# Gated cross-attention block: attention scores with bias kept in their PSUM banks instead of an SBUF score tile

## The reference, cut to what matters

```python
q = jnp.einsum('bfd,dnh->bfnh', x, Wq) * H ** (-0.5)
k = jnp.einsum('btd,dnh->btnh', src, Wk)
v = jnp.einsum('btd,dnh->btnh', src, Wv)
hbias = jax.nn.relu(dist[..., None] @ Wth + bth)
qs_bias = (hbias @ Wto + bto)[..., 0]
logits = jnp.einsum('btnh,bfnh->bnft', k, q)
logits = logits + bias + qs_bias[:, None]
w = jax.nn.softmax(logits, axis=-1)
out = jnp.einsum('bnft,btnh->bfnh', w, v)
```

## Time and profile before

| what | value |
|---|---|
| median of 3 runs | 1392.51 us (1392.48 to 1393.23) |
| span of the profiled execution, first to last instruction | 1391.1 us |
| what lies around the span, against the median | 1.4 us |
| busy share of the span, PE / DVE / ACT / POOL | 90% / 88% / 76% / 60% |
| mean granted TensorE clock over the span | 0.968 |

### The profile page before, as it was taken

How to read it: one execution, slowest core, us unless ns; L and a number is a source line. 1 busy time by engine, 2 the same in 40 slices (tenths; PEclk the granted TensorE clock), 3 DMA queues, 4 the chain that set the end, 5 groups by cost and what they waited for, 6 DMA issues and landing times.

```text
span 1391.1 us, 39815 instructions
## 1 busy us (share of the span) xinstructions
PE 1246.5 (90%) x11184; PEld 1035.3 (74%) x11184; DVE 1221.8 (88%) x4922; ACT 1062.8 (76%) x3353; POOL 833.3 (60%) x889
## 2 busy tenths in 40 slices
PE   1599989898989899998989898989898999799998
PEld 1377878787878787787778787878777877677776
DVE  4899989898989899998989898989898988579886
ACT  4588868787878788787878787868687866478886
POOL 3677767676767677776767676767676753111110
PEclk9799999999999999999999999999999999999999
DMA  5201000102110100021100000111101000000000
GB/s 152 67 7 31 15 27 12 29 12 76 44 31 12 31 12 22 20 67 39 35 16 16 25 13 29 57 48 27 31 12 42 12 12 9 5 23 19 23 14 9
DMA packets 69115, 41.04 MB, mean 30 GB/s; under 512 B 14840, under 2 KB 63872, under 8 KB 68992
## 3 DMA queue, kind: packets, MB, share of 16 engines
q1 hardware_dynamic: 68992, 39.84, 9.9%
HBM read 23.29 MB, written 1.05 MB: 17 GB/s over the span
## 4 chain that ended last, share of the span: by engine, by line
PE 23%; issue 23%; DVE 23%; ACT 18%; POOL 2%; DVEq 1%; DMA 1%; ACTq 0%; SPq 0%; POOLq 0%
ACT prob L802 10%; DVE bias_acc L951 4%; PE L L688 4%; ACT relu_z L785 4%; PE O L552 3%; PE M L582 3%; DVE score L998 3%; DVE qT L1123 3%; DVE hid L1073 3%; PE M L762 2%; DVE st L1016 2%; PE M L628 2%; PE T L695 2%; PE M L560 2%; ACT probT L809 1%
## 5 line engine op out<-in xcount | busy, mean ns | idle before, releaser
L802 ACT ACTIVATE prob<-score,nmax 128x128 f32<-128x128 f32 x1024 | 396.6, 390 | 182.4 <-DVE nmax L998 182.2
L1396 POOL TENSOR_TENSOR prob<-prob,rinv 128x512 f32<-128x512 f32 x256 | 293.5, 1146 | 232.1 <-DVE rinv L1006 229.7
L951 DVE SCALAR_TENSOR_TENSOR bias_acc<-relu_z,cst,bias_acc 128x512 f32<-128x512 f32 x370 | 339.1, 917 | 9.7 <-ACT relu_z L785 0.2
L785 ACT ACTIVATE relu_z<-dist_g,cst 128x512 f32<-128x512 f32 x386 | 295.0, 804 | 17.2 <-DMA cst<-cst_all 16.9
L998 DVE CUSTOM_DVE_ANT_0 score<-L,bias 128x128 f32<-128x128 f32 x1024 | 233.6, 281 | 4.0 <-PE L L528 1.5
L802 ACT ACTIVATION_READ_ACCUMULATOR prob<-score,nmax 128x1 f32 x1024 | 193.3, 189 | 0.0
L1391 POOL TENSOR_TENSOR sd<-mv,half 128x1 f32<-128x1 f32 x128 | 105.5, 824 | 120.3 <-DVE mv L1018 117.6
L538 PE MATMUL T<-ident,prob 128*128 128x128 f32 x1024 | 164.4, 285 | 4.9 <-POOL prob L1396 4.0
L552 PEld LDWEIGHTS O<-probT,v 128*64 128x64 f32 x2048 | 109.3, 136 | 60.0 <-issue 52.4
L582 PE MATMUL M<-wv,ctxT 128*128 128x512 f32 x256 | 144.1, 645 | 7.8 <-DVE hid L1073 5.1
L528 PE MATMUL L<-kT,qT 64*128 64x128 f32 x2048 | 148.7, 285 | 0.0
(11 more groups left out here) (134 smaller groups left out, 2282.8 us busy)
## 6 DMA issues: line engine op xcount, KB each, us to landing
dist_g<-in_fside_BxSxS SPq DMA_DIRECT2D x16, 256.0 KB, 2.8
mask_g<-in_mask_Bx1x1xS_ff SPq DMA_DIRECT2D x16, 256.0 KB, 3.3
ctxT<-ctxT_all SPq DMA_DIRECT2D x64, 64.0 KB, 1.9
xs<-x_all SPq DMA_DIRECT2D x64, 64.0 KB, 1.8
x_all<-xs SPq DMA_DIRECT2D x64, 64.0 KB, 1.8
wk<-in_L_xattn_Wk SPq DMA_DIRECT2D x4, 512.0 KB, 3.6
wv<-in_L_xattn_Wv SPq DMA_DIRECT2D x4, 512.0 KB, 4.7
wq<-in_L_xattn_Wq SPq DMA_DIRECT2D x4, 512.0 KB, 5.1
```

The lines of the kernel that those rows point to most:

```text
L785: nc.scalar.activation(relu_z[:, z_slot(g, k), :], dist_g[:, :, :], ACT.Relu, bias=cst[:, C_BTH + k:C_BTH + k + 1], scale=cst[:, C_WTH + k ...
L802: last = nc.scalar.activation(prob[:, c, m, :], score[:, c, m, :], ACT.Exp, bias=nmax[:, c, m:m + 1], scale=-1.0, accum_out=rsum[:, c, m:m ...
L951: vec.scalar_tensor_tensor(out=bias_acc[:, :], in0=relu_z[:, z_slot(g, k), :], scalar=weight, in1=bias_acc[:, :], op0=ALU.mult, op1=ALU.ad ...
L1396: gp.tensor_tensor(prob[:, c, :, :], prob[:, c, :, :], rinv[:, c, :].rearrange("p (m o) -> p m o", o=1).broadcast_to([P, 4, P]), ALU.mult) ...
```

## The change

The scores with the bias are written back in place, into the bank that they came from; the exponential reads them there; the SBUF tile `score` (8 KB a partition) is gone. PE may write the banks again only when the exponential has read them, so its wait at L524 goes from `scored` to `exp_done`, with the same count.

```diff
-        score = sb("score", [P, QUADS, 4, P])
...
-                wait(pe, scored, after(g, i, 4, 2 * octet - 1))
+                wait(pe, exp_done, after(g, i, 4, 2 * octet - 1))
...
                 for m in range(4):
-                    last = nc.scalar.activation(prob[:, c, m, :], score[:, c, m, :], ACT.Exp, bias=nmax[:, c, m:m + 1],
+                    last = nc.scalar.activation(prob[:, c, m, :], L[c % 2][:, m * P:(m + 1) * P], ACT.Exp, bias=nmax[:, c, m:m + 1],
                                                 scale=-1.0, accum_out=rsum[:, c, m:m + 1])
...
-                    last = vec.tensor_tensor_reduce(out=score[:, c, m, :], in0=L[c % 2][:, m * P:(m + 1) * P], in1=bias[:, i % GROUP, :],
+                    last = vec.tensor_tensor_reduce(out=L[c % 2][:, m * P:(m + 1) * P], in0=L[c % 2][:, m * P:(m + 1) * P], in1=bias[:, i % GROUP, :],
                                                     scale=-1.0, scalar=BIG, op0=ALU.add, op1=ALU.min,
                                                     accum_out=nmax[:, c, m:m + 1])
```

## The result

The changed kernel takes 1406.33 us (median of 4 runs, 1403.92 to 1414.29), the kernel before, run beside it, 1392.49 us (4 runs, 1386.82 to 1393.23). The two medians are 13.8 us apart, which is 1.0%, where 1404 us was predicted. The ratio on record is 1.013, with a 95% interval of 1.0093 to 1.0167: slower beyond noise, but the size of the loss is known only to some 13 to 23 us. Lines of the file after the removed tile are one lower than before: the scores are L527 instead of L528, the exponential L801, DVE's score instruction L997.

What follows compares the result with a forecast made beforehand. DVE was taken to set the pace, PE having about 0.4 us to spare a step. A loss of 0.7 us a group over 16 groups, 11.2 us on 1391.1, plus 1.4, gave 1404 us; 8-in-10 range 1386 to 1440.

Steps and rivals of the forecast that it cites:

- the first half of the mechanism: Before the octet-1 scores: PE stands until ACT's exponentials of quad 1 are done, 0.60 us in every step.
- The terms of the sum: DVE's added standing in steps 0, 1 and 2 of a group: 0.3 + 0.2 + 0.2 = 0.7 us; step 3 nothing.
- five signs: PE idle 0.6 us before octet-1 scores; exponentials 0.35 apart; score instructions 0.21; DVE waiting for `wo`; steps 1, 2 at 16.7.
- The standing of PE: Before the octet-1 scores, PE waits for ACT's exponentials of quad 1: 0.60 us, in every step.
- The exponential from PSUM: ACT's exponentials of a quad: 0.35 us apart instead of 0.39, a gain of 0.04 each, 0.16 a quad.
- DVE's write to PSUM: DVE's score instructions: no change from 0.21 us apart, with -0.04 and +0.04 us an instruction as ends.
- Rival (b): DVE's score write to PSUM is dear: at +0.04 us each, 0.64 us a step, about 1435 us; chance 0.22.
- DVE sets the pace, PE follows with about 0.4 us to spare: In steps of 16.5 us, DVE sets the time; PE is without work for 0.38 and 0.41 us in steps 1 and 2.
- The wait of DVE for `wo`: Before DVE's residual: PE's late projection `wo` makes DVE stand 0.2 us in steps 1 and 2.
- The turn of the loop: In step 3, PE's 4.27 us without work take its lateness away, so the change costs nothing there.
- Rival (a): PE's own 0.4 us of slack a step swallows the moved wait: no difference, 1395 us; chance 0.18.
- Rival (c): DVE's score write to PSUM is cheaper: at -0.04 us each, 11 us faster in all, 1381 us; chance 0.15.

Runs made afterwards that it cites:

- the wait alone: The kernel before, SBUF tile kept, with only PE's wait moved from `scored` to `exp_done`: 1408.97 us against 1391.78, ratio 1.0133.

## Why the prediction was right, point by point, and where it was off

The direction and the first half of the mechanism held: the time came out 2.3 us above the forecast, well inside its range. The terms of the sum did not hold as well. Of the five signs that were to show the forecast right, two came: PE's standing and the shorter exponentials. The score instructions did not stay at 0.21 us, DVE did not wait for `wo`, and the steps came to 16.9 us instead of 16.7.

**The standing of PE** was right in place, releaser and size: 0.57 us measured (row and median), 0.60 predicted, and it came in 63 of 64 units. So was its cause, the loop through `apply`, the copy of `v` and four exponentials: with the exponentials ahead of that copy it is gone.

**The exponential from PSUM**: 0.34 us apart, predicted 0.35. The exponential alone went from 0.292 to 0.249 us (medians, to the start of the accumulator read). The Trainium skill (Perfetto Trace Analysis, Optimizing Scalar/DVE Operations) gives ScalarE an overhead of about 93 ns on SBUF and 51 ns on PSUM; the difference of 42 ns agrees with the 43 ns of these traces.

**DVE's write to PSUM** was taken as no change, with bounds of 0.04 us. That step failed: three writes of four cost the upper bound, which makes 0.11 us a quad (256 quads: 28 us of DVE's time). The nearest rows were those of reads, and they say nothing of a write behind a write. Rival (b) had this price, but with 41 us on the path and PE no longer late; PE was late all the same, only 6.6 us got there without the standing, and beside the standing none can be told. The same section of the Trainium skill has 60 ns for DVE on SBUF and 125 ns on PSUM. The runs disagree: no difference for a PSUM write between SBUF writes, 40 ns for one behind another PSUM write.

**"DVE sets the pace, PE follows with about 0.4 us to spare"** is the step that failed, and here the sum went wrong. The spare time is about right: before the first feed-forward product PE had 0.30 us on average (0.32 in the row). But the forecast took DVE's stream for the pace, let another 0.2 us of overlapping ends come back to PE, and charged a step only the 0.2 us for which DVE would wait for `wo`. What the runs show instead is the closed loop through PE, DVE, PE and ACT: 16.91 us in the changed kernel, 16.92 with the wait alone, whose DVE work is that of before. The prediction had the part of it from `apply` to the scores, but did not follow it on through `wo`, `turn`, the `probT` copy and `hid` back to `apply`. PE's time without work in step 1 went from 0.38 to 0.74 us, which is the new 0.57 and the 0.17 at the second octet of values. Steps 1 and 2 lost 0.41 and 0.40 us instead of 0.2, step 0 0.49 instead of 0.3, together 1.30 instead of 0.7 us a group. The wait of DVE for `wo` that carried the predicted loss appears with the wait alone (47 times), but not in the changed kernel. ACT's gain did shorten PE's standing, but DVE's dearer quad 0, which the forecast had at nothing, gave it back on the same loop.

**The turn of the loop** was taken as unchanged. Eight of the 13 turns are unchanged (21.77 to 22.04 us, before 21.68 to 23.06). The other five take 20.83 to 21.04: in the first row of the stretches above the granted clock is 1.00 throughout (2.4 GHz), in the last it is 0.92, so a part of it runs at the lower level of 1.2 GHz. In turns of both kinds PE stands for 3.2 to 3.4 us. In the kernel before all 13 turns have slowed matmuls behind that stand; with the wait alone four have none. This gives back 0.43 us a group, so 1.30 became 0.86. That the total came within 2.3 us of the forecast is in part luck: two errors of opposite sign, steps that lost 0.6 us a group more than forecast and turns that gained. Why the clock stayed up in these turns was not tried. The kernel's runs scatter over 10 us: three, the profiled one among them, had a mean clock of 0.978, the slowest 0.970 (before, profiled: 0.968).

**Rival (a)**, that the reserve swallows the wait, fell: the 0.32 us before the first feed-forward product did vanish, but 0.57 us of standing came in their place, and steps 1 and 2 went to 16.9 us. **Rival (c)** fell with the price of the write.

## What to carry to other kernels

When a buffer is to be freed later in a chain, look at what its new last reader has queued ahead of that read: here a copy that waited for the same engine which then waited for the buffer, and moving four instructions past it was worth more than the change had cost in any other way. Then follow the waits round until they close, before calling one engine the pace: here a loop through three engines set the step, and none of them alone. Two costs need not add: what lies outside the loop that sets the step is hidden by it. And an engine's busy time bought or sold in small pieces says little: 0.2 us less on DVE was worth 0.03 us in one kernel and 0.11 in another, 0.22 more nothing in one place and half of it in another.

## What the runs showed of the hardware that was not expected

- A DVE instruction that writes PSUM directly behind another that does so takes 0.25 us to the next start instead of 0.21 (both writes in the same bank); alternating with SBUF writes, all take 0.21. The accumulator read behind an instruction with its output in PSUM shows 0.14 us instead of 0.08, at no cost in distance.
- At the turn of the loop DVE's program stands for about 2.7 us without a wait. With one copy a step moved off DVE it stands twice (4.95 us before the first `rinv`), and a turn takes 3.3 us more, more than anything else tried here. No run tested why.
- The same turn takes 21.9 us with a granted clock of 0.92 or 20.9 us at 1.00, in one and the same execution of the changed kernel.
